# Two mixtures of experts in a perceiver kernel: tiles written out, results scattered by token, combines with plain loads

## What is computed

```python
# layer 0: 8 experts, 2 chosen per token, inner width 1024
cw = zeros((T, E)).at[arange(T)[:, None], idx].set(weights)
act = silu(einsum('th,ehf->tef', x, W1) + b1)
y = einsum('tef,efh->teh', act, W2) + b2
out = einsum('te,teh->th', cw, y) + 0.1 * (silu(x @ Ws1 + bs1) @ Ws2 + bs2)
# layer 1: 16 experts, 4 chosen per token, inner width 192, gate and up projection,
# out = sum over the 4 chosen of w * w2(silu(w1 x) * (w3 x)), plus one shared expert
```

## Time and profile before

| | us |
|---|---|
| three runs | 1789.2, 1789.33, 1795.58 (median 1789.33) |
| profiled execution, time | 1790.47 |
| its span | 1788.7 (mean granted clock 0.841) |
| PE, PEld busy | 1312.2 (73%), 969.3 (54%) |
| DVE, ACT, POOL busy | 1123.2 (63%), 778.5 (44%), 458.0 (26%) |
| chain that ended last | POOL 3%, issue 1%; the rest under 1% |

### The profile page before, as it was taken

The page is one execution under the profiler, slowest core; times in us unless marked ns, Lnnn a source line. Parts: engine busy times, 40 slices in busy tenths (PEclk is TensorE's granted clock), DMA queues, the critical chain, the costliest instruction groups (busy, mean ns, idle before and its releaser), DMA issues. The chain is left out here.

```text
span 1788.7 us, 47046 instructions
## 1 busy us (share of the span) xinstructions
PE 1312.2 (73%) x14649; PEld 969.3 (54%) x14650; DVE 1123.2 (63%) x3056; ACT 778.5 (44%) x2056; POOL 458.0 (26%) x591
## 2 busy tenths in 40 slices
PE   4999999966674188599999838998922658888700
PEld 2788888842342178488888623335711436666500
DVE  5899999977998767533333353325578865555433
ACT  6788888843223146443343205214540434444300
POOL 0555555502000300111111050200210024334275
PEclk9999999988787589899999858758955878899855
DMA  3333333210000135311111190870010532222234
GB/s 98 89 80 79 81 79 80 61 51 0 1 0 30 66 102 169 124 39 38 41 38 38 55 308 6 265 255 22 1 63 0 176 104 88 84 90 90 73 106 123
DMA packets 113189, 147.38 MB, mean 82 GB/s; under 512 B 14938, under 2 KB 99107, under 8 KB 113123
## 3 DMA queue, kind: packets, MB, share of 16 engines
q1 hardware_dynamic: 102706, 118.13, 21.6%
q0 software_dynamic: 10272, 28.06, 5.5%
q10 hardware_dynamic: 144, 0.35, 0.1%
HBM read 124.73 MB, written 21.76 MB: 82 GB/s over the span
## 5 line engine op out<-in xcount | busy, mean ns | idle before, releaser
L1177 DVE TENSOR_SCALAR and_attentions_routed_hs<-_and_attentions_routed_h 128x512 f16<-128x512 f32 x78 | 33.2, 426 | 163.2 <-PE ps L1570 158.4
L1563 ACT ACTIVATE _and_attentions_routed_h<-ps,mixture_and_attentions_b 128x128 f32<-128x128 f32 x312 | 89.2, 368 | 98.8 <-PE ps L1557 98.8
L1557 PE MATMUL ps<-xture_and_attentions_x_s,ture_and_attentions_m_wh 128*128 128x128 f16 x1248 | 125.6, 220 | 0.9 <-DVE xture_and_attentions_x_s L1169 0.8
L639 POOL TENSOR_TENSOR ads_and_recurrence_ctx_s<-ads_and_recurrence_ctx_c,ads_and_recurrence_ctx_s 128x512 f16<-128x512 f32 x64 | 74.2, 1159 | 177.3 <-ACT ads_and_recurrence_ctx_s L568 177.3
L588 ACT ACTIVATE ads_and_recurrence_probs<-ps,s_and_recurrence_neg_max 128x257 f32<-128x257 f32 x256 | 117.7, 479 | 1.0 <-DVE s_and_recurrence_neg_max L670 0.9
L1317 PE MATMUL ps<-stage_second_mixture_x_s,tage_second_mixture_m_wh 128*128 128x128 f16 x948 | 103.0, 237 | 1.1 <-issue 1.1
L1387 DVE SCALAR_TENSOR_TENSOR _second_mixture_routed_h<-ps,_second_mixture_routed_h 128x128 f32<-128x128 f32 x79 | 23.1, 292 | 111.7 <-ACT _second_mixture_routed_h L1357 111.7
L1433 POOL DMA_INDIRECT tage_second_mixture_rows<-n_rows,age_second_mixture_row_i x79 | 75.7, 958 | 62.2 <-POOLq L1432 60.6
L1557 PEld LDWEIGHTS ps<-xture_and_attentions_x_s,ture_and_attentions_m_wh 128*128 x1248 | 85.9, 98 | 9.0 <-issue 1.2
L1557 PE MATMUL ps<-xture_and_attentions_x_s,ture_and_attentions_m_wl 128*128 128x128 f16 x624 | 87.9, 220 | 0.0
L679 DVE TENSOR_SCALAR _heads_and_recurrence_pn<-ads_and_recurrence_probs,heads_and_recurrence_inv 128x256 f32<-128x256 f32 x256 | 79.9, 371 | 8.3
(11 more groups left out here) (419 smaller groups left out, 3769.6 us busy)
## 6 DMA issues: line engine op xcount, KB each, us to landing
ads_and_recurrence_ctx_t<-in_ctx_t SPq DMA_DIRECT2D x64, 257.0 KB, 2.7
e_and_attentions_b_ctx_t<-in_ctx_t SPq DMA_DIRECT2D x16, 1028.0 KB, 8.6
xture_and_attentions_raw<-in_m_w SPq DMA_DIRECT2D x32, 512.0 KB, 3.5
ure_and_attentions_b_ctx<-in_ctx SPq DMA_DIRECT2D x32, 512.0 KB
stage_second_mixture_raw<-in_m_w SPq DMA_DIRECT2D x16, 640.0 KB, 5.0
y_rows<-_second_mixture_routed_y SPq DMA_DIRECT2D x79, 128.0 KB, 1.8
ds_and_recurrence_mask_i<-in_mask SPq DMA_DIRECT2D x256, 32.1 KB, 1.7
y_rows<-_and_attentions_routed_y SPq DMA_DIRECT2D x39, 128.0 KB, 1.7
```

The lines of the kernel that those rows point to most:

```text
L639: pool.tensor_tensor(ctx_s[p][1][:, :, :], ctx_c[p][:, :, :], ctx_s[p][0][:, :, :], ALU.subtract).then_inc(k.a_low.sem, 1)
L1557: last = pe.matmul(ps[:, bank + f // 4, (f % 4) * P:(f % 4 + 1) * P], at_block(w, e * mix.blocks + c, f * P, P), a[:, c, :], start=(n == 0 ...
L1563: last = act.activation(h[:, f * P:(f + 1) * P], ps[:, bank + f // 4, (f % 4) * P:(f % 4 + 1) * P], ACT.Silu, scale=1 / (WS * NS), bias=b1 ...
```

## The change

`first_tiles` and `second_tiles` are written out tile by tile on every engine, with constants for waits and buffers. In both, PE interleaves the pieces of `ascend(s + 2)` with those of `descend(s)`; in layer 0 this was one tile ahead and not interleaved, and the halves `hs` get a second buffer. PE (and ACT in layer 0) read the packed experts every sixth tile. In layer 1 shared and routed tiles become one block with 16 + 79 tiles, the weight casts are done by tile 13, `ascend(16)` waits for the last of them, POOL gathers 28 of the 79 tiles ahead into 32 row buffers, and the last product of the descent uses all 128 rows. The gathers take their column of indices straight from `r.token`. Results are no longer stored by SP: POOL scatters each row to row `choice * 2048 + token` of `y_rows` (unused slots to spare rows), with an indirect DMA per tile. The combines load those rows with one plain DMA per token tile on SP, ahead of `fetch` in SP's order, DVE works on two token tiles in turn, and in layer 1 each token tile is stored when it is done; the block with the last store goes. The table's loop is written out with four buffers and summed choice by choice, and some small DVE instructions make token and destination from it.

```diff
-            with pe.Fori(1, NT - 1) as t:
-                for kk in range(K):
-                    add_to_table(t * K + kk, kk % 2, False, False)
...
+            for kk in range(K):
+                for t in range(NT):
+                    u = kk * NT + t
+                    pe.wait_ge(k.m_onehot.sem, k.m_onehot.at(u + 1))
+                    pe.matmul(ps[:, SB, kk * NTL:(kk + 1) * NTL], hot_lo[u % 4][:, :], hot_hi[u % 4][:, :], start=(t == 0), stop=(t == NT - 1)).then_inc(k.m_placed.sem, 1)
...
+def experts_of(k, eng, mix, r, s, n):
+    packed = eng.value_load(r.expert[0:1, s:s + 1], min_val=0, max_val=E1 ** AT_ONCE - 1)
+    return [k.nc.snap((packed >> 4 * j) & (E1 - 1), engines=[eng.engine], min_val=0, max_val=mix.E - 1) for j in range(n)]
...
+            for s in range(N):
+                if not shared and s + 3 < N:
+                    turn(s + 3)
+                for f in range(FC):
+                    if s + 2 < N:
+                        ascend(s + 2, f)
+                    descend(s, f)
...
+            for u in range(N):
+                if NT <= u + 3 < N:
+                    turn(u + 3)
+                for j in range(3):
+                    if u + 2 < N:
+                        ascend(u + 2, j)
+                    descend(u, j)
...
-                pe.matmul(out, h[0:REST, 2, :], at_block(wl[0:REST, :, :], e, DOWN + D, D), start=False, stop=True).then_inc(k.t_down.sem, 1)
+                    pe.matmul(out, h[:, 2, :], at_block(wl, e, DOWN + D, D), start=False, stop=True).then_inc(k.t_down.sem, 1)
...
+        def casts(u):
+            return range(2 * u, 2 * u + 2) if u < 2 else range(u + 2, u + 3) if u + 2 < mix.E else ()
...
-                pool.tensor_copy(idx[b][:, :], r.table[:, bass.ds(s, 1)]).then_inc(k.t_idx.sem, 1)
-                pool.wait_ge(k.t_idx.sem, k.t_idx.at(2 * s + 1))
...
+            def scatter(s):
+                pool.wait_ge(k.t_ycopied.sem, k.t_ycopied.at(s + 1))
+                pool.indirect_dma_start(k.y_rows, bass.IndirectOffsetOnAxis(ap=r.dest[:, s:s + 1], axis=0), y[s % 4][:, :], None).then_inc(k.t_stored[s % 4].sem, 16)
+            gathered = 0
+            for s in range(mix.tiles):
+                while gathered < min(R - 4 + (mix.tiles - R + 4) * (s + 1) // (mix.tiles - 12), mix.tiles):
+                    gather(gathered)
+                    gathered += 1
+                scatter(s)
...
+            chosen = k.y_rows[0:K * T, :].rearrange("(k t p) d -> t p k d", k=K, p=P)
+            for t in range(NT):
+                sp.wait_ge(k.g_added.sem, k.g_added.at(t - 3))
+                sp.dma_start(y[t % 4][:, :, :], chosen[t]).then_inc(k.g_load[t % 4].sem, 16)
+                if out is not None and t >= 4:
+                    store(t - 4)
+            if fetch is not None:
+                fetch(sp)
+            if out is not None:
+                for t in range(NT - 4, NT):
+                    store(t)
...
+                for n in range(K):
+                    for q in pair:
...
+                        last = dve.scalar_tensor_tensor(k.x[:, q, :], y[q % 4][:, n, :], r.w[:, n, q:q + 1], k.x[:, q, :], ALU.mult, ALU.add)
...
-                sp.dma_start(dram["out"].rearrange("(t p) d -> p t d", p=P), k.x[:, :, :]).then_inc(k.out_stored.sem, 16)
```

More of the change, by code:

```diff
@@ new lines, in _ @@
+            if not shared:
+                turn(0)
+                turn(1)
+            for f in range(FC):
+                ascend(0, f)
+            if not shared:
+                turn(2)
+            for f in range(FC):
+                ascend(1, f)
+            for s in range(N):
+                if not shared and s + 3 < N:
+                    turn(s + 3)
+                for f in range(FC):
+                    if s + 2 < N:
+                        ascend(s + 2, f)
+                    descend(s, f)
@@ L1204, in _ @@
+            split(0)
+            split(1)
+            for s in range(N):
+                if not shared and s + 3 < N:
+                    take(s + 3)
+                if s + 2 < N:
+                    split(s + 2)
+                if shared:
+                    add(s)
+                    for q in range(s * F, (s + 1) * F):
+                        cast_low(q)
         @block.sync
         def _(sp):
-            def body(i, s, b, ahead, e):
-                if shared:
-                    for q, w, n in fed(i, s, b):
-                        sp.wait_ge(k.t_wlow.sem, k.t_wlow.at(q - 1))
-                        sp.dma_start(raw[w][:, :], k.dram[f"m{mix.n}_w"][bass.ds(q, 1), :, :].rearrange("o p n -> p (o n)")).then_inc(k.t_raw[w].sem, 16)
-                else:
-                    store(s, b % 2)
@@ new lines, in _ @@
+            gathered = 0
[3 more added lines that the diff above has]
+                    gathered += 1
+                scatter(s)
+            for b in range(4):
+                pool.wait_ge(k.t_stored[b].sem, k.t_stored[b].at((mix.tiles + 3 - b) // 4))
+    for s in (k.t_up, k.t_act, k.t_gated, k.t_high, k.t_low, k.t_down):
+        s.base += N
+    k.t_added.base += NT
@@ L1455, in combine @@
+    for s in (k.t_cast, k.t_wlow):
+        s.base += mix.E
+    for s in (k.t_trans, k.t_xcopied, k.t_ycopied):
+        s.base += mix.tiles
+    for b in range(4):
+        k.t_raw[b].base += mix.E // 4
+        k.t_stored[b].base += (mix.tiles + 3 - b) // 4
+    for s in range(mix.tiles):
+        k.t_rows[s // 4 % 8].base += 1
+def combine(k, mix, r, biases=None, fetch=None, out=None):
     nc, ps, c_ = k.nc, k.ps, k.c
@@ L1505, in _ @@
                 dve.tensor_copy(cw_t[:, :].rearrange("e (g n) -> e g n", g=G), ps[0:E + 1, 0:G, :]).then_inc(k.g_weights.sem, 1)
-            for t in range(NT):
-                x = k.x[:, t, :]
-                if biases is not None and t % 2 == 0:
+            for t in range(0, NT, 2):
+                pair = (t, t + 1)
+                if biases is not None:
                     both = k.x[:, t:t + 2, :].rearrange("p t d -> p (t d)")
```

622 lines of the change are left out of this document (282 added, 340 removed).

## The result

| | before | after |
|---|---|---|
| median of the runs, us | 1789.26 | 1729.43 |
| single runs | 1788.41 to 1795.58 | 1711.51, 1727.89, 1730.96, 1732.01 |
| profiled execution: time, span | 1790.47, 1788.7 | 1727.89, 1725.8 |

The ratio is 0.964 (95% interval 0.957 to 0.971): the change is worth 60 us, not the 107 forecast, and 1729 lies outside the range of 1645 to 1722.

A forecast was written before the change was run, and what follows sets the result against it. No single engine bounds the kernel; PE's queue more than its array paces layer 1's routed tiles. Terms -4 + 0 - 1 - 17 + 10 - 8 - 35 - 52 = -107 us gave 1682 us, range 1645 to 1722.

The forecast's parts named there:

- Table, -4: Table loop written out with four buffers: 0.43 us a unit for 0.495; net -3 and -1 us, bounds -8 and 0.
- Layer 0, shared tiles, 0: Layer 0's shared tiles: a buffer's round of load and casts stays the period; 0 us, between -4 and +4.
- Layer 0, routed tiles, -17: Layer 0's routed tiles: PE's idle gap, mostly at loop turns, goes as a whole; -17 us, bounds -30 and 0.
- Rival 2: Routed tiles: addresses made anew, more register instructions; layer 0 gains nothing, layer 1 at 2.75 us a tile; 1723 us, chance 0.12.
- last scatter and block end 3.6 us: Layer 1, after the last result: 3.6 us assumed for last scatter and block end, before the combine's first load.
- Layer 0, combine, +10: Layer 0's combine and next boundary: the ring's fetch waits behind 16 loads on SP; +10 us, between +3 and +16.
- Layer 1, seam, -8: Layer 1, shared to routed tiles: rows gathered early, first routed ascent about 7 us sooner; -8 us, bounds -10 and -4.
- Layer 1, routed tiles, -35: Layer 1's routed tiles: loop turns -17, 128-row product -16, constant wait counts -2; 2.45 us a tile, bounds -54 and -11.
- POOL at 2.2 us a tile: Layer 1's routed tiles: POOL's gathers and one scatter a tile take 2.2 us, fitting by 10%; scatter taken as 1.25 us.
- POOL beside DVE's casts: Layer 1's gathers: DVE's casts hardly hold them up; by the skill's rule POOL's 2.2 us would exceed PE's 2.45.
- Layer 1, combine and store, -52: Layer 1, last result to end: 96.8 us becomes 44.5, eight pairs at 4.1 us; -52 us, bounds -56 and -35.
- Rival 3, slow loads: Both combines: loads of rows 2 MB apart run at half of 304 GB/s; 1720 us in all, chance 0.06.

The follow-up runs named there:

- second measurement: The changed kernel measured once more with no edit, against the kernel before: 1716.1 us against 1796.7, ratio 0.956 (0.947 to 0.966).

## Why the prediction was wrong

Direction right, size not: 60 us (80 in the second measurement) against 107. By its own steps:

- **Table, -4.** -8.9 us (-3.5 and -5.4). Mis-sized in the good direction: a unit of layer 1's table now takes 0.37 us (63 units from 1382.3 to 1405.7), where I took 0.43, and in layer 0 0.36.
- **Layer 0, shared tiles, 0.** From the start of the stage to the first routed result 131.2 us became 132.7. Right.
- **Layer 0, routed tiles, -17.** -12. The failed step is "interleaving lets the queue run through the descents, where it has time": apart, the tiles are as fast. PE's whole idle time was read as recoverable, 12.3 us of it at the turns, but the turns gave the queue only 5.4 us. Rival 2 had the right resource (register instructions) and the wrong sign of their number.
- **What I left out: POOL's drain at the end of the tiles.** The term "last scatter and block end 3.6 us" in layer 1 measured 12.0, and layer 0 had no such term, where 2.5 became 9.9. The step failed because I took the block's end from a trace in which POOL's last work lay tiles ahead. The rows were there: both combines before end with POOL's drain, 9.5 and 20.3 us long, beside DVE's last adds. Some 15 us, shown by removing it.
- **Layer 0, combine, +10.** +5.1 in the block and +3.7 in the boundary, by the mechanism forecast. Right (a pair was taken as 2.9 us but reckoned with 2.75; the fetch began at 24.0 us). It could have been avoided: moving the fetch one block on gives back 25 us.
- **The attention, no term.** +17 in the profiled execution, +5.5 in the next. It is the time at which its clock falls; my range had nothing for it.
- **Layer 1, seam, -8.** From the block's start to the first result 71.6 us became 65.0: -6.6. Right.
- **Layer 1, routed tiles, -35.** -25. The term that failed is "with 128 rows I expect 3 to be left: -16", which measured -0.5; its 19.4 us of waits lay on the array side while the queue's instructions followed each other at their usual spacing. The turns' -17 was nearly right, -14: the branch and six readings went, and a reading with its decoding costs 1.95 us in place of 1.5. The constants' -2 was far too small: fewer addresses and arithmetic less more waits are -12 of queue time. So the -25 is partly luck: I had a gain where there was none and missed one where there was.
- **POOL at 2.2 us a tile.** It is the next limit, not yet binding: with the addresses gone the tiles stop at 2.14, POOL's queue full. The scatter that no row showed takes as long as a gather:

```profile
L1456 POOL DMA_INDIRECT y_rows<-stage_second_mixture_y,ge_second_mixture_r_dest x79: 969/976/1077, 1474.3 to 1674.7; - x79
```

- **POOL beside DVE's casts.** The forecast said that the 79 gathers of the kernel before ran beside DVE's casts. They did not run beside the casts of the weights: those end at 1451.4 us, the first gather starts at 1452.9. In the changed kernel the early gathers do, and DVE's cast holds them up (timelines of DVE and POOL, and all 79 gathers):

```profile
1426.67 1.48 DVE L1430 SCALAR_TENSOR_TENSOR tage_second_mixture_m_wl<-stage_second_mixture_raw,tage_second_mixture_m_wh 128x1280 f16<-128x1280 f32 x1
...
1427.13 1.85 POOL L1452 DMA_INDIRECT tage_second_mixture_rows<-n_rows,e_second_mixture_r_token  x1 [0.30 <-issue]
...
L1452 POOL DMA_INDIRECT tage_second_mixture_rows<-n_rows,e_second_mixture_r_token x79: 944/983/1852, 1409.4 to 1646.0; - x79
```

  Twelve gathers start while such a cast runs. Each of them ends 0.82 us after the cast's end, whatever its start: nine take 1.85 us, three 1.09 to 1.10. A gather that starts 0.8 us before the cast takes 0.95 us. The Trainium skill, "SBUF — State Buffer", section "SBUF: two separate sides", has the rule that a DVE instruction in two-port mode keeps GpSimd from writing descriptors; the trace agrees that DVE holds gathers up, though it does not name the cast's mode. POOL stands still for 21 us behind these early gathers, so the delay is not on the path. The scatters start after the casts, beside DVE instructions of under 0.4 us, and the longest is 0.1 us over the median.
- **Layer 1, combine and store, -52.** From the last result to the end 96.8 us became 51.7, -45; without the drain 43.7 (1652.0 to 1695.7), -53. Right but for the block's end (the forecast's parts add up to 44.1, not 44.5).
- **Rival 3, slow loads.** The combine's loads, with rows 2 MB apart from choice to choice, ran at 264 GB/s, the stores included. The Trainium skill, "DMA: Bandwidth & Descriptors", section "Latency and other measured facts", gives 164 GB/s for a row pitch of 2 MiB; as read in the forecast, that pitch is not this one.

## What to carry to other kernels

A block that ends with an indirect DMA on POOL pays for POOL's drain, some 6 to 9 us here, though the data has landed; look at the DRAIN rows of the line that opens the block, and at which engine's work comes last after the edit. Where an instruction takes its address from a register, count the register instructions of the queue at their spacing, not at their length, before crediting any idle time of the array. And when a block's end is set by what a queue issues, ask whether the next block could issue it.

## What the runs showed of the hardware

- POOL's drain after an indirect DMA: it ended 8.1 and 10.2 us after the last scatter's record, of which POOL's waits for the landing take 1.6 and 1.8 us. What POOL still does then was not found out.
- A register instruction in PE's queue costs 0.112 us of the queue at a recorded length of 0.032 us.
- A gather on POOL that starts while DVE casts the weights (1.48 us) ends 0.82 us after the cast, so it takes up to 1.85 us in place of 0.95.
- The time of one and the same attention block lies between 102 and 119 us from execution to execution, with its granted clock between 0.67 and 0.51.
